# A vision transformer block on one core: queries and keys packed two heads to a row group, and one reordering

## What is computed

```python
q = (x @ w_q.T + b_q).reshape(Bn, Tn, H, HD)      # H = 12, HD = 16
k = (x @ w_k.T + b_k).reshape(Bn, Tn, H, HD)
v = (x @ w_v.T + b_v).reshape(Bn, Tn, H, HD)
scores = jnp.einsum('bqhd,bkhd->bhqk', q, k) * scale + mask[None, None]
attn = jax.nn.softmax(scores, axis=-1)
ctx = jnp.einsum('bhqk,bkhd->bqhd', attn, v).reshape(Bn, Tn, Dn)
return ctx @ w_o.T + b_o
```

## Time and profile before

| | us |
|---|---|
| median of 3 runs | 166.53 |
| lowest and highest of them | 165.94, 167.59 |
| the profiled execution, its own time | 166.45 |
| its span, from the first to the last instruction | 164.6 |
| TensorE (PE) busy | 147.1 |
| VectorE (DVE) busy | 116.2 |
| ScalarE (ACT) busy | 89.7 |
| GpSimd (POOL) busy | 42.0 |

### The profile page before, as it was taken

The page is one execution under the profiler, slowest core; times in us unless marked ns, Lnnn a source line. Parts: engine busy times, 40 slices in busy tenths (PEclk is TensorE's granted clock), DMA queues, the critical chain, the costliest instruction groups (busy, mean ns, idle before and its releaser), DMA issues.

```text
span 164.6 us, 4269 instructions
## 1 busy us (share of the span) xinstructions
PE 147.1 (89%) x1717; PEld 113.5 (69%) x1717; DVE 116.2 (71%) x285; ACT 89.7 (54%) x198; POOL 42.0 (26%) x55
## 2 busy tenths in 40 slices
PE   0449999999989998979998999999899999999992
PEld 0217778863658997868645677888668788788781
DVE  6299969799897678957673797785885832732753
ACT  0498797561679335453457697655465343334440
POOL 0000001000000000000000345368576677487330
PEclk9999999999999999999997899999999999999998
DMA  5999974900000000002995000258000000000003
GB/s 142 387 361 381 300 190 100 415 19 0 0 0 4 4 4 4 4 0 67 378 405 210 0 0 0 63 207 329 2 4 0 0 4 2 2 4 0 0 0 111
DMA packets 7391, 16.89 MB, mean 103 GB/s; under 512 B 800, under 2 KB 3612, under 8 KB 7372
## 3 DMA queue, kind: packets, MB, share of 16 engines
q1 hardware_dynamic: 7012, 16.29, 28.5%
q10 hardware_dynamic: 360, 0.34, 0.7%
HBM read 16.15 MB, written 0.47 MB: 101 GB/s over the span
## 4 chain that ended last, share of the span: by engine, by line
PE 57%; DVE 24%; ACT 7%; issue 6%; ACTq 3%; POOL 2%; DVEq 0%; POOLq 0%
PE PS L590 19%; PE PS L618 11%; PE PS L436 4%; PE PS L323 3%; PE PS L344 2%; PE PS L346 2%; PE PS L410 2%; PE PS L347 2%; DVE mx L1123 2%; DVE xsq L1127 2%; DVE hn L1064 2%; PE PS L455 2%; DVE vhl L1268 2%; PE PS L310 2%; POOL vhl L876 1%
## 5 line engine op out<-in xcount | busy, mean ns | idle before, releaser
L885 POOL TENSOR_TENSOR kq<-vhl,kq 128x296 f16<-128x296 f32 x35 | 29.4, 841 | 87.0 <-ACT kq L837 86.8
L1268 DVE SCALAR_TENSOR_TENSOR vhl<-PS,vhl 128x296 f32<-128x296 f32 x36 | 16.8, 466 | 21.9 <-POOL vhl L876 12.1
L830 ACT ACTIVATE vhl<-PS 128x296 f32<-128x296 f32 x36 | 15.0, 416 | 26.5 <-PE PS L590 26.4
L837 ACT ACTIVATE kq<-vhl 128x296 f16<-128x296 f32 x36 | 16.0, 445 | 5.4 <-DVE vhl L1268 5.4
L876 POOL TENSOR_TENSOR vhl<-vhl,xs 128x296 f32<-128x296 f32 x14 | 12.6, 900 | 5.6 <-issue 4.8
L1257 DVE TENSOR_TENSOR vhl<-vhl,xs 64x296 f32<-64x296 f32 (+1 forms) x18 | 10.2, 565 | 2.8 <-ACT vhl L830 2.6
L590 PE MATMUL PS<-XAh,piece 128*128 128x296 f16 x48 | 10.8, 310 | 0.3
L590 PE MATMUL PS<-XAh,slab 128*128 128x296 f16 x48 | 10.0, 291 | 0.9 <-DVE vhl L1268 0.9
L344 PE MATMUL PS<-whl,xhl 128*128 128x193 f16 (+1 forms) x40 | 10.6, 266 | 0.0
L346 PE MATMUL PS<-whl,xhl 128*128 128x193 f16 (+1 forms) x40 | 10.6, 265 | 0.0
L347 PE MATMUL PS<-whl,xhl 128*128 128x192 f16 (+1 forms) x40 | 10.5, 262 | 0.0
(11 more groups left out here) (215 smaller groups left out, 395.3 us busy)
## 6 DMA issues: line engine op xcount, KB each, us to landing
slab<-in_w_inner_dram SPq DMA_DIRECT2D x3, 960.0 KB, 9.5
xs<-gate_rows_dram SPq DMA_DIRECT2D x8, 296.0 KB, 5.9
xs<-in_x_inner_dram SPq DMA_DIRECT2D x3, 592.0 KB, 10.6
stage<-in_f_a_dram SPq DMA_DIRECT2D x2, 768.0 KB, 4.8
stage<-in_f_b_dram SPq DMA_DIRECT2D x2, 768.0 KB, 6.4
stage<-in_f_d_dram SPq DMA_DIRECT2D x2, 576.0 KB, 7.9
xhl<-in_f_a_dram SPq DMA_DIRECT2D x1, 768.0 KB, 8.8
xhl<-in_f_b_dram SPq DMA_DIRECT2D x1, 768.0 KB, 10.3
```

Source lines behind the costliest of these rows:

```text
L830: A(silu[:, i % 2, :], PS[:, 3 + 2 * (i % 2), 0:HALF], ACT.Silu, scale=1.0 / XW).then_inc(S["a_silu"], 1)
L837: A(ah[:, f % ABUF, half * HALF:(half + 1) * HALF], hf[:, i % 3, :], ACT.Copy).then_inc(S["a_ah"], 1)
L885: G.tensor_tensor(al[:, f % ABUF, cols], hf[:, i % 3, :], ah[:, f % ABUF, cols], ALU.subtract).then_inc(S["g_al"], 1)
L1268: V.scalar_tensor_tensor(out=hf[:, i % 3, :], in0=PS[:, 4 + 2 * (i % 2), 0:HALF], scalar=SH / XW, in1=src[:, i % 2, :], op0=ALU.mult, op1= ...
```

## The change

Groups 0 and 1 of queries share one product: a lane of 32 rows now holds the 16 dimensions of a head of group 0 and, below, the 16 of a head of group 1 (QA, KA). Group 2 keeps its doubled form (QB, KB). To keep the two heads apart in the scores, keys of the shared product are written to K32 twice, once with the odd 16 rows scaled to zero (`keven`) and once with the even ones (`kodd`); both scales are columns that VectorE makes from a constant. That makes 8 QKV outputs of five products instead of 12. The weights are packed while they are cast: five ScalarE instructions per part (four of 64 columns, in runs of 16, and one of 256), and then one of 393 for each part; VectorE's low parts of queries and keys follow the same five pieces. f = 0 to 3 are taken pass by pass ahead of the transposes, and 4 to 7 are half 1. ScalarE takes kq_high(0) (two instructions) and kq_high(1), then high_parts part 1, and then the rest. VectorE takes low_parts part 1 directly behind the values' low parts, ahead of ffn_low(0, 0). The scores keep their number of products; QKS is doubled and the divisor halved.

```diff
 def kq_product(f):
-    half, r = divmod(f, 6)
-    return r // GROUPS, r % GROUPS, half
+    half, r = divmod(f, 4)
+    return r // 2, r % 2, half
...
+        def lane_cols(w, slot):
+            return w.rearrange("p (r s d) -> p s r d", r=LANES, s=2)[:, slot]
+        def head_cols(rows, k, q, g):
+            raw = awst[rows, k, (KC if q else QC) + g * P:(KC if q else QC) + (g + 1) * P]
+            return raw.rearrange("p (r c d) -> p c r d", r=LANES, c=2)[:, 0]
+        def third_cols(rows, k):
+            return awst[rows, k, 0:VC].rearrange("p (q c) -> p q c", q=2)[:, :, 2 * P:3 * P]
...
-            pe.wait_ge(S["a_aw"], 1)
+            pe.wait_ge(S["a_aw"], 5)
...
-                c0 = (QC if q else KC) + g * P
-                if f in (0, 6):
+                c0 = ((KA, KB), (QA, QB))[q][g]
+                if f in (0, 4):
                     tokens_ready(0, half, i)
...
             for passes in ((0, 1), (2,), (3,), (4,)):
-                for f in range(3):
+                for f in range(4):
                     for i in passes:
                         kq_pass(f, i)
             transposes(0, (1, 2, 0), (3, 4))
-            for f in range(3, 12):
-                if f >= 4:
-                    q4, g4, half4 = kq_product(f - 4)
-                    pe.wait_ge(S["a_q" if q4 else "a_k"], GROUPS * half4 + g4 + 1)
+            for f in range(4, 8):
+                q, g, _ = kq_product(f)
+                pe.wait_ge(S["a_q" if q else "a_k"], g + 1)
                 for i in range(5):
                     kq_pass(f, i)
...
-                                          Q32[rows, g, tok], K32[rows, g, tok], start=False, stop=True,
+                                          Q32[rows, g // 2, tok], K32[rows, g, tok], start=False, stop=True,
...
             act.wait_ge(d_aw, 80)
-            A(WAh[:, :], awst[:, 0, :], ACT.Copy, scale=SW).then_inc(S["a_aw"], 1)
-            A(WB[:, :], awst[:, 1, :], ACT.Copy, scale=SW).then_inc(S["a_aw"], 1)
-            A(WC[:, :], awst[0:CROWS, 2, :], ACT.Copy, scale=SW).then_inc(S["a_aw"], 1)
+            for k, (W, rows) in enumerate(((WAh, slice(0, P)), (WB, slice(0, P)), (WC, slice(0, CROWS)))):
+                for q in (0, 1):
+                    for g in (0, 1):
+                        A(lane_cols(W[rows, (QA, KA)[q]:(QA, KA)[q] + P], g), head_cols(rows, k, q, g), ACT.Copy,
+                          scale=SW).then_inc(S["a_aw"], 1)
+                A(third_packed(W[rows, QB:VP]), third_cols(rows, k), ACT.Copy, scale=SW).then_inc(S["a_aw"], 1)
+            for k, (W, rows) in enumerate(((WAh, slice(0, P)), (WB, slice(0, P)), (WC, slice(0, CROWS)))):
+                A(W[rows, VP:PW], awst[rows, k, VC:AW], ACT.Copy, scale=SW).then_inc(S["a_aw"], 1)
...
+                if f == 0:
+                    act.wait_ge(S["v_jm"], 11)
                 if q:
                     A(Q32[:, g, cols], PS[:, 3 + f % 4, 0:HALF], ACT.Copy, scale=QKS / XW).then_inc(S["a_q"], 1)
+                elif g == 0:
+                    A(K32[:, 0, cols], PS[:, 3 + f % 4, 0:HALF], ACT.Copy, scale=keven[:, :])
+                    A(K32[:, 1, cols], PS[:, 3 + f % 4, 0:HALF], ACT.Copy, scale=kodd[:, :]).then_inc(S["a_k"], 1)
                 else:
-                    A(K32[:, g, cols], PS[:, 3 + f % 4, 0:HALF], ACT.Copy, scale=1.0 / XW).then_inc(S["a_k"], 1)
+                    A(K32[:, 2, cols], PS[:, 3 + f % 4, 0:HALF], ACT.Copy, scale=0.5 / XW).then_inc(S["a_k"], 1)
...
             kq_high(0)
             kq_high(1)
+            high_parts(0, (1, 2, 0), 1)
             kq_high(2)
-            high_parts(0, (1, 2, 0), 1)
-            for f in range(3, 12):
+            kq_high(3)
+            ffn_high(0, 2)
+            for f in range(4, 8):
                 kq_high(f)
-                if f in (5, 8):
-                    ffn_high(0, 2 + (f - 5) // 3)
-            ffn_high(0, 4)
-            ffn_high(0, 5)
+            for q in range(3, 6):
+                ffn_high(0, q)
...
+            dve.wait_ge(d_cst, 16)
+            V.tensor_scalar(kodd[:, :], kscale, -1.0 / SK, None, ALU.mult).then_inc(S["v_jm"], 1)
+            V.tensor_scalar(keven[:, :], kscale, 1.0 / SK, 1.0 / XW, ALU.mult, ALU.add).then_inc(S["v_jm"], 1)
+            def queries_keys_low(k):
+                W, hi, rows = low_of[k]
+                dve.wait_ge(S["a_aw"], 5 * k + 5)
+                for q in (0, 1):
+                    c0 = (QA, KA)[q]
+                    for g in (0, 1):
+                        V.scalar_tensor_tensor(out=lane_cols(W[rows, c0:c0 + P], g), in0=head_cols(rows, k, q, g),
+                                               scalar=SW, in1=lane_cols(hi[rows, c0:c0 + P], g), op0=ALU.mult,
+                                               op1=ALU.subtract).then_inc(S["v_awl"], 1)
+                V.scalar_tensor_tensor(out=third_packed(W[rows, QB:VP]), in0=third_cols(rows, k), scalar=SW,
+                                       in1=third_packed(hi[rows, QB:VP]), op0=ALU.mult,
+                                       op1=ALU.subtract).then_inc(S["v_awl"], 1)
...
             low_parts(0, (1, 2, 0), 0)
             normed(0, (3, 4))
             for k in range(3):
-                attention_low(k, VC, AW)
+                values_low(k)
+            low_parts(0, (1, 2, 0), 1)
             ffn_low(0, 0)
             thrice(0, 0)
             thrice(1, 0)
-            low_parts(0, (1, 2, 0), 1)
             thrice(2, 0)
             thrice(3, 0)
```

More of the change, by code:

```diff
@@ L47 @@
 AW = RC + 9
+QA, KA, QB, KB, VP = 0, 128, 256, 384, 512
+RP = VP + RC - VC
+PW = RP + 9
 CROWS = 97
@@ L146, in vit_kernel @@
         awst = sb("awst", [P, 3, AW])
-        WAh, WAl, WB = (sb(n, [P, AW], F16) for n in ("WAh", "WAl", "WB"))
-        WC = sb("WC", [CROWS, AW], F16)
+        WAh, WAl, WB = (sb(n, [P, PW], F16) for n in ("WAh", "WAl", "WB"))
+        WC = sb("WC", [CROWS, PW], F16)
+        kodd = sb("kodd", [P, 1])
+        keven = sb("keven", [P, 1])
         KFC = 2 * LANES * 4 * BLOCK
@@ L434, in values @@
                     xr = [x[:, (2 * i + b) * BLOCK:(2 * i + b + 1) * BLOCK] for x in (RAh, RAh, RB, RAl, RC_)]
-                    for k, (w, x) in enumerate(zip(wparts(VC, VC + D), xr)):
+                    for k, (w, x) in enumerate(zip(wparts(VP, VP + D), xr)):
                         last = mm(PS[0:BLOCK, (7, 0, 1, 2)[i % 4], b * D:(b + 1) * D], x, w,
@@ L516, in _ @@
             pe.wait_ge(S["v_jr"], 2)
-            pe.wait_ge(S["a_k"], 6)
-            pe.wait_ge(S["a_q"], 6)
+            pe.wait_ge(S["a_k"], 4)
+            pe.wait_ge(S["a_q"], 4)
             scores(0)
@@ L564, in router @@
                     tok = slice(t * P, (t + 1) * P)
-                    for k, (x, w) in enumerate(zip(yparts(tok, CROWS), wparts(RC, RC + 9))):
+                    for k, (x, w) in enumerate(zip(yparts(tok, CROWS), wparts(RP, RP + 9))):
                         mm(PS[:, 7, 9 * t:9 * t + 9], x, w, start=(t == 0 and k == 0), stop=False,
                            skip_group_check=True)
-                    last = mm(PS[:, 7, 9 * t:9 * t + 9], XO[:, :], WC[:, RC:RC + 9], start=False, stop=True,
+                    last = mm(PS[:, 7, 9 * t:9 * t + 9], XO[:, :], WC[:, RP:RP + 9], start=False, stop=True,
                               skip_group_check=True)
@@ L787, in exps @@
                     act.wait_ge(S["p_pt"], 2 * u - 2)
-                A(prob[:, u % 2], sdif[:, u % 2], ACT.Exp, scale=1.0 / (8 * QKS)).then_inc(S["a_exp"], 1)
+                A(prob[:, u % 2], sdif[:, u % 2], ACT.Exp, scale=1.0 / (4 * QKS)).then_inc(S["a_exp"], 1)
             A(vv[:, :, :, GROUPS * HD:VW].rearrange("p b r o -> p (b r) o"),
@@ L963, in _, with values_low @@
             V.tensor_tensor(mk[two[1], :], mkf[two[1], :], mk[two[1], :], ALU.subtract).then_inc(S["v_mk"], 1)
-            def attention_low(k, c0, c1):
-                W, hi, rows = ((WAl, WAh, slice(0, P)), (WB, WB, slice(64, P)), (WC, WC, slice(96, CROWS)))[k]
-                dve.wait_ge(S["a_aw"], k + 1)
-                V.scalar_tensor_tensor(out=W[rows, c0:c1], in0=awst[rows, k, c0:c1], scalar=SW, in1=hi[rows, c0:c1],
+            dve.wait_ge(d_cst, 16)
+            V.tensor_scalar(kodd[:, :], kscale, -1.0 / SK, None, ALU.mult).then_inc(S["v_jm"], 1)
+            V.tensor_scalar(keven[:, :], kscale, 1.0 / SK, 1.0 / XW, ALU.mult, ALU.add).then_inc(S["v_jm"], 1)
+            low_of = ((WAl, WAh, slice(0, P)), (WB, WB, slice(64, P)), (WC, WC, slice(96, CROWS)))
+            def queries_keys_low(k):
[10 more added lines that the diff above has]
+                                       op1=ALU.subtract).then_inc(S["v_awl"], 1)
+            def values_low(k):
+                W, hi, rows = low_of[k]
+                dve.wait_ge(S["a_aw"], 16 + k)
+                V.scalar_tensor_tensor(out=W[rows, VP:PW], in0=awst[rows, k, VC:AW], scalar=SW, in1=hi[rows, VP:PW],
                                        op0=ALU.mult, op1=ALU.subtract).then_inc(S["v_awl"], 1)
@@ L982, in _ @@
```

(2 more changed lines are left out.)

14 lines of the change are left out of this document (8 added, 6 removed).

## The result

Over 20 runs of each, the median fell from 166.52 to 164.5 us; the ratio is 0.988 with an interval of 0.986 to 0.991, which is 1.6 to 2.3 us. The forecast was 164.3. Four of the changed kernel's 20 executions ran longer (166.4 to 170.2 us) with a fallen clock, and the ratio leaves such executions out. The profiled execution took 165.14 us, with a span of 163.3.

The account below looks back on a forecast made before the run. TensorE's product count and VectorE's order were taken as the bound; values start 2.24 us earlier (1.39 products, 0.85 order), front hidden: 166.45 - 2.24 = 164.2, plus 0.08 for the median, 164.3 us; range 163.6 to 166.0.

Parts of the forecast that it names:

- The products: TensorE's QKV products: 60 become 40, 2.53 us less; without the new order only 1.39 us would be gained.
- The order: VectorE's XAl and XC ahead of the feed-forward split: gives the other 0.85 us of the 2.24.
- ScalarE between the halves: ScalarE's copies, then XAh and XB: f=0 read twice, XB done at 46.49, 0.37 us later than before.
- The pointer scale: Per-partition scale operand of ScalarE's K copies: put at nothing, upper price 0.1 us in each of two.
- Passing through: Values to row maximum: shifts whole to 54.33; VectorE's own_values let it go at 54.25, margin 0.08 us.
- So the whole 2.24 arrives: Behind the row maximum: every wait is relative to the one before, so the full 2.24 us reaches the end.
- The front: Weight casts and low parts: ScalarE +1.0 us, VectorE +0.5 us, both hidden by waits of 1.66 and 0.71 us.
- B: Front shows: small casts or low parts don't overlap, up to 1.5 us late, 165.8, half of it 165.0; chance 0.15.
- E: Slower: VectorE's 64-column strided low parts cost 0.44 us each without overlap, L1020 3.8 us late, 168.1; chance 0.06.
- D: Clock falls after TensorE's new holes (0.75 and 0.3 us), costing 1.7 us: 166.0; chance 0.06.
- C: Gain ends on VectorE, likeliest through the double K copy ahead of XB: loses 0.5 to 0.8, 165.0; chance 0.09.
- F: XB so late that the low parts' move gains nothing; only the products' 1.39 us left, 165.1; chance 0.04.

Follow-up runs that it names:

- e11: Changed kernel with low parts of tiles 3 and 4 back behind the split and two replications (products only), second run: 165.71 us, ratio 0.997.
- e1: Kernel before, 12 QKV outputs kept, only the low parts of tiles 3 and 4 moved ahead of the feed-forward split: 165.38 us, ratio 0.994.
- e3: Changed kernel with ScalarE's high parts of tiles 3 and 4 (XAh, XB) ahead of the copy of f=1: 164.14 us, ratio 0.987.
- e4: Changed kernel with both copies of each shared key product scaled by one constant, heads not kept apart: 163.80 us (one run).
- e6: Changed kernel padded with 24 products of 8 columns in place of 4 keep-warm products of 512 columns: 163.79 us, ratio 0.987.
- e10: The padded changed kernel of e6 again: 164.18 us, ratio 0.989.
- e5: Changed kernel with 15 more small VectorE low parts into spare tiles, ahead of L1020: 166.77 us, ratio 1.000 to before.
- e2: Changed kernel with low parts of tiles 3 and 4 back behind the split (products only), first run, clock fell: 165.63 us, ratio 0.995.
- e0: Changed kernel run again unchanged, as yardstick; the clock fell in its profile: 164.90 us, ratio 0.990.
- e7: Changed kernel with queries ahead of keys, earlier transposes, half 1 in pairs, high parts behind one copy, later VectorE splits: 164.00 us, ratio 0.986.
- e9: Changed kernel a third time, unchanged, beside the padded one: 164.31 us, ratio 0.990.

## Why the prediction was right

**The products.** The forecast for TensorE's half 0 was exact: 2.52 us from the first product to the transposes (43.00 to 45.52), 2.51 forecast. Alone, the products were worth 1.26, not 1.39: from the 48.03 release on the old kernel had 27 products left and the packed one 17, so ten fewer, where the prediction took eleven.

**The order.** On top of the products it gave 0.72 (from e11's 7.85 to 7.13) where 0.85 was forecast. Alone it gave 1.08, where e1's expectation had 0.86: the 0.2 more is XC's, which TensorE had also waited for. The holes that fewer products leave, because XB on ScalarE is then late, were in the forecast (1.3 us of them); e3 confirms their cause.

**ScalarE between the halves.** This is the term that was mis-sized. The pointer scale was "put at nothing, since starts and not durations set the queue", with 0.1 us in each of two copies as the upper price. It cost 0.09 in each: the starts moved apart as well. e4 gives the 0.18 back to the hundredth. With it the values came 7.13 and not 6.87 us behind the first product; most of the other 0.08 is that the first value product stands 0.15 us behind the end of the fourth replication (49.98 to 50.13), where 0.04 was forecast. The Trainium skill (ScalarE: Activation LUTs, "What ACT_TABLE_LOAD costs") says that each pointer operand adds about 93 ns to an ACTIVATE; the durations here agree (0.51 against 0.42).

**Passing through.** The margin of 0.08 us on VectorE was just used up: own_values ended at 55.05 in after and the scores were done at 55.02. Row maximum 12.06, forecast 11.8.

**"So the whole 2.24 arrives"** was wrong as a step, and that the end came out near the forecast is in part luck: one term of 0.53 against it and one of 0.37 for it, neither foreseen, nearly cancel. Two things behind the row maximum moved that no wait of this chain explains: the pause of 0.53 us on TensorE, and the root that VectorE waits 0.37 less for. The first goes away when products are added ahead of it (e6, e10). For the second I have only the rows: the wait is 0.71 us in before and in e1, and 0.34 in every profile of a packed kernel, so it goes with the packing and not with the order. From the row maximum to the end that makes 108.03 and 108.06 us in before and e1, and 107.73 to 107.75 in the packed kernels without the pause. Why the packing does it was not tested.

**The front.** ScalarE's casts took 3.95 us, forecast 4.24; VectorE's part 3.23, forecast 3.5, since a small instruction costs 0.13 us to the next one and not 0.15. In the profile of after all of it was hidden, with 0.80 us to spare. In the four profiles with early patches ScalarE's longer list was not: 0.15, 0.37, 0.38 and 0.77 us late. The prediction took one execution's 1.66 us of ScalarE's waiting, and 0.71 of VectorE's, for a cover that is always there. So a small part of B did come, in some executions, through ScalarE's `hn`; over the 11 packed profiles without e5 it is 0.15 us on the mean. B in full would have needed casts or low parts that don't overlap. E falls: it would have needed 0.3 us per small instruction. In after, the first piece for partitions 64 and up starts at 29.27, 0.03 us behind the end of the one before it, while inside a part they overlap; that is the hold that the row of L969 had shown. It comes twice among the 15 low parts (at 29.27 and 30.28), not three times.

**The clock (D).** Not in the profile of after, but it is real: behind two holes of 0.85 and 0.97 us in e2, and behind one of 0.80 in e0. I had priced a fall at 1.7 us; e2's values came 1.33 us later than e11's and its row maximum 1.65. C came to 0.02 us: the double copy ahead of XB was late by 0.18, but VectorE's queue added next to nothing to that. F fell with e11 and e3.

## What to carry to other kernels

Removing products pays only as far as the operands of the next ones are there: read what releases the first product behind the cut, and move that producer ahead in its engine's queue in the same change; here either alone gave a little over half of what both gave (1.26 and 1.08 of 1.98 us). A scale that arrives as a column instead of a constant cost 0.09 us of start distance in each copy here, and both stood on the path. When profiles of two versions are compared, count from a common instruction behind the front, since the scatter ahead of it (L1020 came anywhere between 31.5 and 32.7) would have blurred every one of the effects above. And look at the front in more than one profile, since a wait that covers it in one execution can be gone in the next.

## What the runs showed of the hardware that I had not expected

TensorE can pause in the middle of a stream of ready products: 0.51 to 0.80 us, behind the same product in eight profiles (after, e0, e3, e4, e5, e7, e9, e11) of kernels with the same number of products ahead of it, and in none of the three padded ones. In e2's profile, whose TensorE program is the same, it was absent; there the clock had fallen earlier. What it waits for isn't visible in the profile. The profile lists 13 transfers of 16 KB in a queue of kind "instruction"; through attention they stand 4 to 5 us apart (in after at 64.8 and 69.5, in e10 at 63.4 and 67.4, in e2 at 65.3 and 69.9), and none falls into the pause. A supply of instructions that comes late would fit the padding's effect, but nothing here tests it.

Behind two holes of under 1 us each, with 0.5 us of work between them, the granted clock fell in one of two profiles (e2, not e11). Five of e2's twelve executions have the same mean clock of 0.99 as the profiled one, and one of e11's twelve (0.989).

Within a part, a 64-column instruction stood 0.13 us ahead of the next on VectorE and 0.15 on ScalarE, so 12 of them cost 1.6 and 1.8 us, not the 2.7 and 2.9 that their durations (0.22 and 0.24) suggest.
